# Value products always in pairs and six buffers of exponentials in the self attentions of a two-layer decoder

## What is computed

```python
scores = jnp.einsum('bhqd,bhkd->bhqk', q, k) * (1.0 / np.sqrt(hd)) + bias[None]   # L0_attn: ALiBi, half the heads forward, half backward
attn = jax.nn.softmax(scores, axis=-1)
out = jnp.einsum('bhqk,bhkd->bqhd', attn, v)
...
attn = jax.nn.softmax(scores / jnp.sqrt(jnp.float32(HEAD_DIM)), axis=-1)          # L1_attn: all keys
...
scores = jnp.where(causal, scores, jnp.asarray(-1000000000.0, h.dtype))           # inside L1_ffn (_mla): causal
```

## Time and profile before

| what | value |
|---|---|
| median of 3 runs | 2472.88 us (2472.33 to 2482.2) |
| the profiled execution, its own time | 2489.75 us |
| its span, first to last instruction | 2488.0 us |
| mean granted clock of TensorE in it | 0.88 |
| PE busy | 2008.7 us, 81% |
| DVE busy | 1277.7 us, 51% |
| ACT busy | 1003.3 us, 40% |
| first, second and third attention | 272, 414 and 270 us |

### The profile page before, as it was taken

One profiled execution on the slowest core, in us unless ns is written; L12 is line 12 of the kernel. 1 busy time (PEld: TensorE's weight loads), 2 busy tenths in 40 slices (PEclk: granted clock), 3 DMA queues, 4 the chain that ended last, 5 costly groups with the idle time before them and its releaser, 6 DMA issues.

```text
span 2488.0 us, 34626 instructions
## 1 busy us (share of the span) xinstructions
PE 2008.7 (81%) x11182; PEld 1038.3 (42%) x11183; DVE 1277.7 (51%) x2034; ACT 1003.3 (40%) x1922; POOL 459.6 (18%) x752
## 2 busy tenths in 40 slices
PE   6599998688439999954899999878778999816990
PEld 3244444334416666622222222344344444514660
DVE  2377773686402222234788888445557777321114
ACT  3136665376101111122366666635433666402320
POOL 2121111421150000043100000132241111241004
PEclk9579999699669999977799999979888999858995
DMA  5653314322721001036211130243153331052213
GB/s 141 147 141 56 56 29 95 75 47 63 256 103 32 30 30 34 25 109 139 43 31 27 27 52 1 63 113 63 30 131 64 53 53 28 22 192 65 63 57 103
DMA packets 126462, 179.70 MB, mean 72 GB/s; under 512 B 33607, under 2 KB 98439, under 8 KB 123015
## 3 DMA queue, kind: packets, MB, share of 16 engines
q1 hardware_dynamic: 120194, 161.32, 27.3%
q0 software_dynamic: 6144, 16.79, 2.1%
HBM read 110.44 MB, written 54.03 MB: 66 GB/s over the span
## 4 chain that ended last, share of the span: by engine, by line
PE 62%; issue 12%; DVE 9%; POOL 8%; SPq 3%; DMA 3%; ACT 3%; POOLq 0%; DVEq 0%; another core or an unknown queue 0%; ACTq 0%; PEldq 0%
PE psum L1407 10%; PE psum L1931 10%; PE psum L1365 10%; PE psum L1389 9%; PE psum L1950 7%; DVE arena L1467 3%; POOL slot_rows L1854 2%; PE psum L957 2%; PE psum L1941 2%; PE psum L920 2%; POOL arena L795 1%; PE psum L1392 1%; PE psum L1368 1%; ACT arena L1448 1%; PE psum L1422 1%
## 5 line engine op out<-in xcount | busy, mean ns | idle before, releaser
L1467 DVE TENSOR_REDUCE arena<-psum 128x1 f32<-128x1024 f32 (+7 forms) x608 | 649.5, 1108 | 167.8 <-PE psum L1365 83.0
L1448 ACT ACTIVATE arena<-psum 128x512 f32<-128x512 f32 (+1 forms) x1120 | 573.3, 590 | 375.9 <-PE psum L1392 189.3
L1365 PE MATMUL psum<-arena 96*128 96x512 bf16 (+7 forms) x1280 | 371.6, 370 | 46.2 <-DMA arena<-k_parts 17.4
L1389 PE MATMUL psum<-arena 99*128 99x512 bf16 (+7 forms) x1280 | 364.4, 353 | 9.5 <-ACT arena L1448 6.7
L1407 PE MATMUL psum<-arena 128*32 128x512 f32 (+3 forms) x2560 | 281.4, 538 | 1.0 <-ACT arena L1448 1.0
L1931 PE MATMUL psum<-arena 128*128 x780 | 269.2, 493 | 2.0 <-ACT arena L1985 1.2
L1365 PEld LDWEIGHTS psum<-arena 96*128 96x128 bf16 (+1 forms) x1280 | 104.7, 100 | 287.3 <-DVE arena L1467 112.8
L2035 DVE COPY arena<-psum 128x640 f32<-128x640 f32 (+1 forms) x78 | 59.1, 758 | 293.2 <-PE psum L1941 293.2
L1389 PEld LDWEIGHTS psum<-arena 99*128 99x128 bf16 (+1 forms) x1280 | 123.2, 98 | 164.3 <-ACT arena L1448 73.5
L1950 PE MATMUL psum<-arena 128*128 (+1 forms) x780 | 189.0, 384 | 2.1 <-DVE arena L2038 1.2
L1931 PEld LDWEIGHTS psum<-arena 128*128 128x128 f32 x780 | 143.6, 192 | 81.5 <-issue 24.2
(11 more groups left out here) (180 smaller groups left out, 2415.5 us busy)
## 6 DMA issues: line engine op xcount, KB each, us to landing
arena<-k_parts SPq DMA_DIRECT2D x144, 128.0 KB
q_halves<-arena SPq DMA_DIRECT2D x80, 192.0 KB
arena<-q_halves SPq DMA_DIRECT2D x40, 384.0 KB, 4.8
arena<-arena SPq DMA_DIRECT2D x48, 256.0 KB, 2.3
arena<-q_halves SPq DMA_DIRECT2D x40, 256.0 KB, 5.2
arena<-slot_rows SPq DMA_DIRECT2D x78, 128.0 KB, 2.0
slot_out<-arena SPq DMA_DIRECT2D x78, 128.0 KB, 1.7
k_parts<-arena SPq DMA_DIRECT2D x48, 192.0 KB
```

The lines of the kernel that those rows point to most:

```text
L1365: last = nc.tensor.matmul(dst[:, base + lo:base + hi], q[0:rows, qh, h, qb % 4 * P:qb % 4 * P + P], k[0:rows, h, key0 + lo:key0 + hi], sta ...
L1389: last = nc.tensor.matmul(b[:, at0:at0 + width], kk[0:rows, h, kb * P:kb * P + P], q[0:rows, qh, h, c0:c1], start=True, stop=diag is None)
L1448: nc.scalar.activation(probs[k % 4][:, heads[0]:heads[-1] + 1, c0:c1], bank[st_bank[no % 3]][:, 0:len(heads) * width].rearrange("p (h q) - ...
L1467: nc.vector.tensor_reduce(dst, src, AX.X, ALU.max).then_inc(t("taken"), 1)
```

## The change

`self.pair` is 2 in all three attentions. There are six buffers of exponentials in place of four: `probs` gets `floor_t` and the 2048 words from `floor_base`, which are free in these stages; ACT's wait and the index of the buffer follow, and `plan` may put scores up to six steps ahead of the value products. In `plan` the due time of value products is later, 3.0 lengths of a step in place of 1.6.

```diff
--- before.py
+++ after.py
@@ -54,6 +54,7 @@
 STK = HD * sum(n for n, m in PARTS)
 FIRST_MAX = 2
 NPLACE = 4
+NPROB = 6
 EARLY = 3
 
 
@@ -109,7 +110,7 @@
         self.groups = [(s, i) for i in (0, 2, 1, 3) for s in range(2)]
         self.jobs = [(g, qh) for g in range(len(self.groups)) for qh in range(2)]
         self.modes = [modes[s] for s, i in self.groups]
-        self.pair = 1 if modes[0] == "full" else 2
+        self.pair = 2
         self.steps, self.job_start, self.spans = [], [], []
         for g, qh in self.jobs:
             self.job_start.append(len(self.steps))
@@ -180,7 +181,7 @@
             if n_st < len(st):
                 k, n = st[n_st]
                 j = self.steps[k][0]
-                if j in landed:
+                if j in landed and len(pvs) > k - NPROB:
                     ready.append((max(landed[j], exps[n_st - 3] if n_st > 2 else 0.0), at[k] + n * took[k] / HG, "ST"))
             if n_mx < len(mx):
                 _, j, n = mx[n_mx]
@@ -197,7 +198,7 @@
                 j = self.steps[n_pv][0]
                 if len(exps) >= done and (j == 0 or len(copied) >= j):
                     ready.append((max(exps[done - 1], copied[j - 1] if j else 0.0), 
-                                  at[n_pv + self.pair - 1] + 1.6 * took[n_pv + self.pair - 1], "PV"))
+                                  at[n_pv + self.pair - 1] + 3.0 * took[n_pv + self.pair - 1], "PV"))
             open_now = [(k, r, w) for r, k, w in ready if r <= now + 0.05]
             if open_now:
                 _, _, what = min(open_now)
@@ -209,7 +210,7 @@
                 j, _, c0, c1, diag, first, end = self.steps[k]
                 free["PE"] = when + score[k] * len(self.spans[k][n]) / HG
                 width = len(self.spans[k][n]) * (c1 - c0)
-                free["ACT"] = max(free["ACT"], free["PE"] + 0.2, pvs[k - 4] if k > 3 else 0.0) + 0.16 + width / 1200
+                free["ACT"] = max(free["ACT"], free["PE"] + 0.2, pvs[k - NPROB] if k >= NPROB else 0.0) + 0.16 + width / 1200
                 exps.append(free["ACT"])
                 self.events.append(("ST", k, n))
                 n_st += 1
@@ -1280,7 +1281,8 @@
                 return sem(f"att_{n}")
 
             probs = [prob[:, 0], prob[:, 1]] + [w2_high[:, n * HG * 512:(n + 1) * HG * 512]
-                                                .rearrange("p (h q) -> p h q", h=HG) for n in range(2)]
+                                                .rearrange("p (h q) -> p h q", h=HG) for n in range(2)] + \
+                [floor_t, arena[:, floor_base:floor_base + HG * 512].rearrange("p (h q) -> p h q", h=HG)]
             st_bank, o_bank = (4, 5, 6), 7
             last_step = [at.job_start[j + 1] - 1 for j in range(len(at.jobs))]
             ng = len(at.groups)
@@ -1405,7 +1407,7 @@
                 pe.wait_ge(t("p"), exps_before(k + 1))
                 for h in range(HG):
                     last = nc.tensor.matmul(bank[o_bank][32 * h:32 * h + 32, c0:c1], v_st[g % 2][:, kb, h, :],
-                                            probs[k % 4][:, h, c0:c1], start=first, stop=end)
+                                            probs[k % NPROB][:, h, c0:c1], start=first, stop=end)
                 last.then_inc(t("pv"), 1)
 
             def pe_move_max(pe, j):
@@ -1440,13 +1442,13 @@
             def act_prog(act):
                 for k, (j, kb, c0, c1, diag, first, end) in enumerate(at.steps):
 
-                    wait(act, t("pv"), k - 3)
+                    wait(act, t("pv"), k - NPROB + 1)
                     for n, heads in enumerate(at.spans[k]):
                         no = at.spans_before[k] + n
                         width = c1 - c0
                         act.wait_ge(t("st_ps"), no + 1)
                         nc.scalar.activation(
-                            probs[k % 4][:, heads[0]:heads[-1] + 1, c0:c1],
+                            probs[k % NPROB][:, heads[0]:heads[-1] + 1, c0:c1],
                             bank[st_bank[no % 3]][:, 0:len(heads) * width].rearrange("p (h q) -> p h q", q=width),
                             ACT.Exp, scale=QSCALE).then_inc(t("p"), 1)
```

## The result

The changed kernel takes 2487.76 us (median of 8 runs, 2483.93 to 2494.42); the kernel before takes 2473.91 beside it (8 runs, 2472.33 to 2482.2). The ratio is 1.0054, with an interval of 1.0039 to 1.0069: slower by 13 us, the interval being 10 to 17. The forecast was 2488, by +15. The profiled run of the changed kernel took 2484.78 us, its span is 2483.0 at a mean granted clock of 0.884.

What follows compares the result with a forecast made beforehand. PE was taken as the bound, with VectorE having only 3.9 us per job to spare. The second attention's +12.2 us and the others' +3 made +15 on the median 2472.88: 2488 us, range 2468 to 2501.

Steps and rivals of the forecast that it cites:

- The switches saved: Second attention: 64 pairs each save 0.24 us of PE's tiling-mode switches, 15.4 us of PE work gone.
- The waits: Second attention: PE waits 2.51 us per job, up from 0.81, mainly for VectorE to free two PSUM places.
- The last ten steps: End of the second attention, no maxima left: five pairs at 5.19 us against 4.80 for two single steps, +2.0 us.
- The second attention: Whole stage: +10.2 us for steps beside maxima and +2.0 for the last ten steps, together +12.2 us.
- 14.6 jobs at 0.7: Second attention, 117 of 128 steps beside maxima: each job grows by 0.7 us, +10.2 us.
- The first and third attention: Pairs standing closer together cost VectorE time: together +3 us, between -5 and +10.
- over its seven such rounds that is +1.3: Third attention: a twelve-step round walked at 31.3 us, with 1.5 us of waits; seven rounds cost +1.3 us.
- the value for the first: First attention, no round walked: bounded by a gain of 3 and a loss of 6, taken as +1.5 us.
- The sum: Whole kernel: 12.2 + 3 = +15 us on the median 2472.88, giving 2488 us.
- The rival that the gain stands: Whole kernel: PE is busiest, so its saved work shortens the kernel by 15.4 us, to 2457; chance 0.09.
- ACT's wait: Second attention's walked rounds: ScalarE is in the way only once, 0.08 us.
- The marker: Second attention's profile: idle time of the maxima's matmuls (L1365) put down to VectorE rises from 7 to over 25 us.

Runs made afterwards that it cites:

- e3: Changed kernel with VectorE taking each maximum of the second attention over only the first 512 of 1024 keys: 2468.34 us in one run.
- e2: Kernel before with only value products paired in the second attention, four buffers and due time 1.6 kept: 2490.42 us, ratio 1.0048.
- e7: Kernel before with due time 3.0 for 1.6, four buffers, single steps in the second attention, scores at most four steps ahead: 2465.66 us, ratio 0.9931.
- e4: Changed kernel with a hand-written order of PE products in jobs 1 to 13 of the second attention: 2502.78 us, ratio 1.0104.
- e8: Changed kernel with another hand-written order in jobs 1 to 13 of the second attention, turning the maxima (MT) earlier: 2485.73 us, ratio 1.0004.
- e10: Changed kernel again without edits, beside the kernel before on the same chip: 2496.45 us, ratio 1.0045.

## Why the prediction was right, and where not

**The switches saved** (15.4 us): right. PE's work per job fell by 0.90 us for the 0.96 that four pairs make; over 16 jobs that would be 14.4 us. The price, read off two neighbouring rows, holds. The Trainium skill says in "TensorEngine Tiling (Array Packing)", section "Key Properties", that a change of tiling mode drains TensorE; the trace agrees in so far as fewer changes took less time, 0.90 us per job, and doesn't show the drain itself.

**The waits** (2.51 per job): right, 2.47, and at the same places, 0.39 and 0.24 in the round that was walked. Job 24.87 forecast with one more digit, 24.87 measured. What made this possible is that nearly every event there stands at distances which repeat to 0.01 us. The waits of before, 0.81 in the text, are 0.91: both sides of the difference were a little off, and the job's growth of 0.7 was 0.66.

**The last ten steps** (+2.0): the pair's distance was right, 5.21 for 5.19. But of the two intervals that hold these steps, 22.18 and 18.72 us before, the last shrank to 17.58 and the other was 22.19 in one profile and 23.81 in the other: -1.1 or +0.5 together, not +2.0. I had summed the pairs' distances and not the end itself. **The second attention** came to +10.2 in one pair of profiles and +12.3 in the other, for +12.2. That it is so close is partly luck. Its parts are 13 jobs in the middle, +8.9 us (0.68 each), the start, +2.3 or +2.9, and the end, -1.1 or +0.5. The forecast had 14.6 jobs at 0.7, +10.2, nothing for the start, and +2.0 for the end: the start, which it left out, stood in for what the end didn't cost.

**The first and third attention** (+3): wrong, also in sign. In the two pairs of profiles they gave back 4.2 and 2.2 us, of which the third has 2.5 and 2.6. The first has -1.7 and +0.4, and that is within its spread: in six profiles with the old order there it took 267.7 to 270.9 us, in six with the changed one 268.3 to 270.2, most of the spread being ahead of its second job. So for the whole of the first no change is shown, though its end is shorter in each of them. The third took 268.3 to 270.4 us in the former six and 266.5 to 268.9 in the latter. The step that failed is "over its seven such rounds that is +1.3", and the value for the first that leaned on it. The third's round takes 31.13 us, not 31.3, for 31.11 before, so seven of them add 0.1 us: there the walk set a wait that isn't there. What I left out are the ends, where no maxima are left. They come out shorter with the new order; that a pair behind more ST is pure gain there fits, but no run isolates it. The last three intervals of the third, 19.85, 7.28 and 14.50 us, are 19.49, 6.54 and 13.92 after; those of the first, 19.70, 16.73 and 4.65, are 20.05, 16.15 and 3.56: 1.7 and 1.3 us less. In the third another 1.7 comes off the first job (18.71 to 17.03), of which 0.8 is given back ahead of its first pair. I walked the end of the second attention, but of these two only the middle.

**The sum** was right to a few us, with an error of +5 to +7 in that term, which the traces show. With -2 to -4 in it the sum would have been +8 to +10; measured were +13.3 (10 to 17) and +11 (8 to 15). The three stages themselves grew by 6.0 and 10.1 us, for the +15 forecast. So the sign, the mechanism in the second attention and the size of its job were foreseen; that 2487.76 lies within 0.3 us of 2488 is luck.

**The rival that the gain stands** was rightly placed low, but its condition was wrong: "It would be right if DVE's maxima were under about 0.9 us each". At 0.69 us (e3) the job still had 1.5 us of waits, for ScalarE and its three banks. The text had counted ACT's wait once, 0.08 us, and not asked how late it would be if VectorE weren't later. The Trainium skill says in "Perfetto Trace Analysis", section "Identifying the Most-Contended Engine", to optimize the engine with the highest occupancy first, but to judge TensorE's headroom by MFU (the share of its peak that its matmuls reach) and by the busy share of its weight loads, since matmul busy time is not a good measure. Here matmuls are busy for 81% of the span, weight loads for 42% and VectorE for 51%, so the rule does not clearly name PE, and these traces don't decide for or against it. What they show is that 0.9 us less of PE's work per job made the job longer.

**The marker** in PE's matmuls, "from 7 to over 25 us", was wrong in its view: 6.9 to 10.0. In weight loads it is 48.1 to 102.8.

**Left out altogether**: what the due time does to single steps. I asked it only for pairs, where e2 against the change shows nearly nothing, and so didn't see that one number of the change, alone, is worth 0.7% (e7).

What stays open: why the first comparison of the two kernels has +13.3 and the second +11 where the stages give +10 on one chip. The intervals overlap, and +10 lies in both; how often an execution meets the low clock at the maxima's end, which is worth 1.6 us, is known only for the profiled ones. Nor is shown whether an order exists in which pairs beat single steps; two orders are too few.

## What to carry to other kernels

Work taken off the busiest engine can be a loss if the engines that read from it through a few PSUM places can't stand its longer absence: walk one period with start-to-start distances, for *each* reader, and through the start and the end of the stage as well as its middle. Try the scheduling constant by itself before the structural change that it comes with. Compare stages, not spans, when two profiles may be from different chips.

## What the runs showed of the hardware that I had not expected

- The same last stretch took 339 to 342 us on one chip and 347 to 350 on two others, at a granted clock of 0.78 and 0.77, with the same number of instructions; medians of the same kernel differed by 10 us (2476 and 2486). The attentions agree between chips to 1.3 us for the kernel before, to 2.3 for the changed one.
- From the turning of the maxima on PE to their rows' arrival by DMA, 5.3 us pass. Before and after leave only 1.2 and 0.7 us more than that.
- A wait of PE of some 1.3 us, at the same place, was followed by a full clock in one profile (the change's first) and by some 3 us at the 1.2 GHz level in three (e4, e8, e10), worth 1.6 us each. Of the 13 waits of 1.5 us in e4's jobs four were followed by such a fall and nine were not.
- The end of a 512-column matmul is drawn so late that a wait of 0.24 us behind it has no bracket; only the starts, or the weight loads, show it.
